# A Mamba layer's inputs computed half by half, with the pair matrix placed by transfers

## The chip, the cores and the metric

The kernel runs on one core of a Trainium2 chip. The metric is the device time of one execution in microseconds, median of the runs shown. Engine names in the rows: PE is TensorE's products and PEld its weight loads, DVE is VectorE, ACT is ScalarE, POOL is GpSimd, SP issues transfers.

## The reference, cut to what matters

The model is a four-layer decoder on x of shape (8, 128, 128), each layer an attention-like part, a cross part and a feed-forward part. The change lies in the first part of the first layer, a Mamba block on the twice-normed x, and in the lines that share its buffers. What it computes, with 256 inner channels, 64 states and a convolution of four taps:

```
xi, z = split(xn @ W_in)                   # 256 channels each
u     = silu(conv4(xi) + conv_b)
dt, B, C = split(u @ W_xproj)              # 8, 64, 64 columns
delta = softplus(dt @ W_dt + b_dt)
A     = -exp(A_log)
h_t   = h_{t-1} * exp(delta_t * A) + (delta_t * u_t) * B_t     # for each channel and state
y_t   = sum over states of h_t * C_t  + u_t * D
out   = (y * silu(z)) @ W_out
```

## The kernel before

Everything runs as blocks: within a block each engine has its own list of instructions, ordered against the others by semaphores written out by hand, and a block ends when all engines have come to its end. There is no planner. Features lie on partitions, the 1024 tokens (8 sequences of 128) on columns; `halves` are 512 columns, one PSUM bank; `IC` is 2, the two groups of 128 channels.

`start_stage` (L251) issues seven loads on SP: X, the Mamba weights `mamba_pack` (1056 KB, the identity among its columns), and five that are needed later (`row_pack`, `CT`, `CTOK`, `rel`, `mask8`). VectorE waits for X and for the whole pack, casts the identity to bf16, and the block ends.

`mamba_stage` (L1006) first norms x twice in one block (`Norm`, L299): VectorE takes statistics and scales, GpSimd takes the power -0.5, TensorE runs bf16 products that nobody reads (`keep_awake`, eight at the first statistics of each norm) and then transposes, VectorE and ScalarE copy one half each into `XNT`.

`mamba_inputs` (L1054) is the block that makes u, gate, delta, du = delta * u, B and C. TensorE's order: four inner products for both halves into banks `Xp` (copied by ScalarE into `padded`, L1148), the second channel group's convolution as four diagonal products a half (`Gp`, L1118), then for each half the dt, B and C products (L1130) and the step products (`Dp`, L1137), and last the gates (L1109 again, into `Gp`). VectorE does the first group's convolution (L1191, L1194) and the softplus, written as max(delta, 0) + ln(1 + e) with a correction. The softplus goes pass by pass over both halves: L1203 twice, then ScalarE's Exp twice (L1172), L1207 twice, Ln twice (L1175), and then L1210, L1213, L1214 and the product with u, L1217, for one half after the other. GpSimd makes the diagonals, adds XN to X (L1227), clears `Cz` (L1228), and builds `A_pairs` (L1231): A times a 0/-1 pattern, so that a product of 32 partitions picks one channel. SP stores du's first half to a scratch tensor in DRAM (L1092), waits, loads the first seven tiles back, spread over partitions (`Spread.load`, L1049, two transfers a tile), and stores the second half.

`scan_block` (L1236) runs 128 tiles, each 128 partitions by 1024. For each: TensorE multiplies delta by `A_pairs` into PSUM (L1331), ScalarE takes Exp (L1445), GpSimd multiplies the loaded du tile by B (L1303), VectorE scans (L1489), and TensorE sums states with `Cz` (L1349). The tiles use a ring of seven areas: `XN`, `XNT`, `O`, `masked_cos`, `masked_sin` and two halves of `pos_bias`. SP loads a tile when the scan seven before it is done. At the end ScalarE widens the mask into `O` (L1457), GpSimd makes the masked tables, and SP loads `pos_bias` (L1291). Later layers use semaphores of their own (`Tally`).

Of the kernel before, what the change touches and what calls it, by code (L numbers as in the profile page):

```python
# [24 lines left out]
T = B * S  # L25
HALF = 512
# [77 lines left out]
def layout(name_shapes):  # L104

    table, at = {}, 0
    for name, n in name_shapes:
# [7 lines left out]
         ("W_out", IC * D), ("pair_rows", 2 * QUADS), ("order", 128), ("alternate", 128)]  # L115
# [25 lines left out]
class Model:  # L141


    def __init__(self, nc, ctx, dram):
# [35 lines left out]
        self.loaded_small = sem("loaded_small")  # L180
# [27 lines left out]
        self.tallies = {}  # L208

    def tally(self, name):  # L210

        if name not in self.tallies:
            self.tallies[name] = Tally(self.sem(f"moe_{name}"))
        self.tallies[name].base = self.tallies[name].n
        return self.tallies[name]
# [35 lines left out]
def start_stage(nc, m):  # L251

    d = m.dram
    with nc.Block() as block:
        @block.sync
        def _(sp):
            sp.dma_start(m.X[:], d["x"]).then_inc(m.loaded_x, 16)
            sp.dma_start(m.mamba_pack[:], d["mamba"]).then_inc(m.loaded_mamba, 16)
            sp.dma_start(m.row_pack[:], d["rows"].to_broadcast([128, ROWS_N])).then_inc(m.loaded_rest, 16)
            sp.dma_start(m.CT[:], d["ctx_feat"]).then_inc(m.loaded_rest, 16)  # L260
            sp.dma_start(m.CTOK[:], d["ctx_tok"]).then_inc(m.loaded_rest, 16)
            sp.dma_start(m.rel[:], d["rel_pos"]).then_inc(m.loaded_rest, 16)
            sp.dma_start(m.mask8[:], d["mask"].to_broadcast([128, T])).then_inc(m.loaded_rest, 16)
# [16 lines left out]
        def _(dve):  # L280
# [8 lines left out]
            dve.wait_ge(m.loaded_mamba, 16)  # L289
            nc.vector.tensor_copy(m.identb[:], m.w("ident"))  # L290

# [7 lines left out]
class Norm:  # L299
# [6 lines left out]
    def __init__(self, nc, m, ctx, src, dst, weight=None, bias=None, ps=None, turn=True):  # L306
        n = m.n_norm
        m.n_norm += 1
        self.turn, self.n_turned = turn, m.n_norm_turned
# [8 lines left out]
    def emit(self, block, complete=None):  # L318
# [48 lines left out]
        def _(pe):  # L367
            pe.wait_ge(m.stats_ready, 2 * n + 1)
            keep_awake(nc, m, ps[:, HALF:], 8)
# [636 lines left out]
def mamba_stage(nc, m):  # L1006

    with ExitStack() as ctx:
        ps = ctx.enter_context(nc.psum_tensor("norm_ps", [D, T], F32))
        first = Norm(nc, m, ctx, m.X, m.XN, ps=ps, turn=False)  # L1010
        second = Norm(nc, m, ctx, m.XN, m.O, m.w("ln_w"), m.w("ln_b"), ps=ps)
        norm_again(m, ctx.enter_context(nc.Block()), first, second)
    with ExitStack() as outer:
        sb = lambda name, shape, dt=F32: outer.enter_context(nc.sbuf_tensor(name, shape, dt))
        u, gate, delta, du = (sb(name, [128, IC, T]) for name in ("u", "gate", "delta", "du"))
        A = sb("A", [128, IC, STATE])
        A_pairs = sb("A_pairs", [128, IC, QUADS, 2, STATE])
        D_order = sb("D_order", [128, IC, 128])
        B2, C2 = sb("B2", [128, T]), sb("C2", [128, T])
        Cz = sb("Cz", [128, S, 32])  # L1020
        du_stored = [m.sem(f"du_stored{h}") for h in range(2)]
        spread = Spread(m)
        mamba_inputs(nc, m, u, gate, delta, du, A, A_pairs, D_order, B2, C2, Cz, du_stored, spread)
        scan_block(nc, m, u, gate, delta, du, A_pairs, D_order, B2, C2, Cz, du_stored, spread)


class Spread:
# [12 lines left out]
    def place(k):  # L1040

        return k // 16, k // 8 % 2, k % 2, k % 8 // 2

# [8 lines left out]


def mamba_inputs(nc, m, u, gate, delta, du, A, A_pairs, D_order, B2, C2, Cz, du_stored, spread):  # L1054
# [5 lines left out]
    with ExitStack() as ctx:  # L1060
# [8 lines left out]
        DTp = ps("DTp", RANK)  # L1069
# [6 lines left out]
        a_ready, diagonal_ready, turned_taps, x_added = (  # L1076
            m.sem(f"mamba_{n}") for n in ("a_ready", "diagonal_ready", "turned_taps", "x_added"))
# [9 lines left out]
        def _(sp):  # L1087
            def store(h):
                sp.wait_ge(du_ready, h + 1)
                for c in range(IC):  # L1090
                    rows = m.dram["du_rows"][h * HB:(h + 1) * HB, c, :, :].rearrange("b r t -> r b t")
                    sp.dma_start(rows, du[:, c, cols[h]].rearrange("r (b t) -> r b t", b=HB)).then_inc(du_stored[h], 16)  # L1092

            store(0)
            sp.wait_ge(x_added, 1)
            sp.wait_ge(g_done, 2 * IC)
            sp.wait_ge(du_stored[0], 16 * IC)
            for k in range(len(spread.areas)):
                spread.load(sp, k)
            store(1)  # L1100

        @block.tensor
        def _(pe):
            def project(ps, at, h, done):
                for c in range(IC):
                    if h:
                        pe.wait_ge(x_copied if at == 0 else g_copied, c + 1)
                    weight = W_in[:, at + c * 128:at + (c + 1) * 128]
                    nc.tensor.matmul(ps[c][:], weight, m.XNT[:, cols[h]], start=True, stop=True).then_inc(done, 1)  # L1109

            for h in halves:
                project(Xp, 0, h, x_done)
            pe.wait_ge(diagonal_ready, TAPS)
            pe.wait_ge(pads_ready, IC)
            for h in halves:
# [5 lines left out]
            for h in halves:  # L1121
# [1589 lines left out]
```

## Time and profile before

| | us |
|---|---|
| median of 3 runs | 1265.73 |
| lowest, highest | 1265.58, 1271.51 |
| span of the profiled execution | 1288.7 |

The span is from the first to the last instruction of the execution that was profiled; of that execution no other time is given. The page shows TensorE busy for 80% of it, VectorE 65%, GpSimd 45% and ScalarE 41%, over stages with different limits, so a stage has to be read by itself. In the rows of a timeline the columns are start, duration, engine, line, operation, output<-inputs, sizes and count, and in brackets the idle time before with what ended it. SPq rows are SP issuing transfers. An f32 product of 512 columns shows as two records.

### The profile page before, as it was taken

The page shows a single profiled execution, that of the slowest core. Times are in us where ns is not written, and L with a number is a line of the kernel's source. Part 1 is how long each engine was busy: PE and PEld are TensorE (multiplying, and loading weights), DVE is VectorE, ACT ScalarE, POOL GpSimd, SP SyncE. Part 2 cuts the span into 40 slices and gives each one's busy share as a digit, 9 for nine tenths or more (in the row PEclk, how much of TensorE's full clock was granted, in tenths as well). Part 3 has the DMA queues.
Part 4 walks back from the last instruction along what each step waited for, and adds up shares of the span by engine and source line. Part 5 has one row for each costly group of instructions (what it writes and reads, how often), then busy time and mean ns, then how long its engine had stood idle before and what let it go on. Part 6 is the DMA issues. An engine that isn't in the chain of part 4 may idle for free. (4 is left out here: it accounts for less than half of the span.)

```text
span 1288.7 us, 30057 instructions
## 1 busy us (share of the span) xinstructions
PE 1028.3 (80%) x12227; PEld 718.2 (56%) x12237; DVE 841.0 (65%) x1508; ACT 525.7 (41%) x1329; POOL 574.0 (45%) x393
## 2 busy tenths in 40 slices
PE   6538877887889999998365798899497999957895
PEld 2127666666774555555265355655377455533795
DVE  5469999999896775567322787487322788855233
ACT  2534444444443742552132274175144577502121
POOL 3389999999964613101435310110524321002232
PEclk9859999999899999999588899899689899978898
DMA  2198899998875000000473000000465000003792
GB/s 114 45 226 213 233 232 230 224 223 228 211 224 190 2 1 1 1 2 1 114 205 110 20 2 1 1 1 2 162 183 192 1 2 2 1 1 95 254 305 83
DMA packets 74376, 139.77 MB, mean 108 GB/s; under 512 B 8144, under 2 KB 28384, under 8 KB 73888
## 3 DMA queue, kind: packets, MB, share of 16 engines
q1 hardware_dynamic: 70272, 129.67, 36.0%
q0 software_dynamic: 3968, 8.18, 1.8%
q8 instruction: 97, 1.59, 0.5%
q14 instruction: 39, 0.32, 0.1%
HBM read 128.06 MB, written 14.82 MB: 111 GB/s over the span
## 5 line engine op out<-in xcount | busy, mean ns | idle before, releaser
L888 ACT ACTIVATE shifted_a<-scores,nmax_a 128x128 f32<-128x128 f32 x768 | 208.6, 389 | 77.4 <-DVE nmax_a L832 75.9
L1445 ACT ACTIVATE decay<-decay 128x1016 f32<-128x1016 f32 x128 | 124.0, 1002 | 152.5 <-PE decay L1331 152.4
L832 DVE TENSOR_REDUCE nmax_a<-scores 128x4 f32<-128x512 f32 x192 | 123.6, 686 | 69.6 <-PE scores L718 67.4
L364 POOL TENSOR_TENSOR rstd<-ve,neghalf 128x4 f32<-128x4 f32 x30 | 31.5, 1051 | 255.9 <-DVE ve L349 255.9
L1331 PE MATMUL decay<-delta,A_pairs 32*128 32x127 f32 x2048 | 83.3, 300 | 75.4 <-DVE small_pack L1489 34.0
L1785 POOL DMA_INDIRECT results<-xs_s x76 | 72.9, 960 | 120.9 <-DVE xs_s L1960 114.5
L838 DVE COPY PTs_a<-PT 128x512 f32<-128x512 f32 x192 | 123.1, 682 | 2.6 <-PE PT L728 2.6
L1331 PEld LDWEIGHTS decay<-delta,A_pairs 32*128 32x128 f32 x2048 | 69.7, 201 | 94.9 <-DVE small_pack L1489 39.4
L728 PE MATMUL PT<-mamba_pack,shifted_a 128*128 128x128 f32 x768 | 106.3, 280 | 4.4 <-DVE PTs_a L838 2.6
L728 PEld LDWEIGHTS PT<-mamba_pack,shifted_a 128*128 128x128 f32 x768 | 82.3, 141 | 30.3 <-issue 19.2
L1303 POOL TENSOR_TENSOR pos_bias<-pos_bias,B 128x1024 f32<-128x1024 f32 x36 | 85.4, 2407 | 1.9 <-DMA pos_bias<-du_rows 1.9
L718 PE MATMUL scores<-KH_a,QT_a 32*128 32x512 f32 x256 | 72.1, 640 | 0.0
L674 POOL TENSOR_TENSOR KH_a<-KT_a,small_pack 128x512 f32<-128x512 f32 x24 | 25.3, 1060 | 99.4 <-PE scores L718 87.6
L1349 PE MATMUL Y<-h,Cz 128*32 128x64 f32 x2048 | 62.1, 288 | 2.9 <-issue 2.1
L1349 PE MATMUL Y<-small_pack,Cz 128*32 128x64 f32 x2048 | 62.4, 288 | 1.4 <-issue 1.4
L1960 DVE TENSOR_SCALAR xs_s<-Y_s,xs_s 128x128 f32<-128x128 f32 x76 | 25.9, 348 | 55.2 <-PE Y_s L1822 26.4
L747 PEld LDWEIGHTS PO<-PTs_a,V 128*32 128x32 f32 x1280 | 30.1, 109 | 53.6 <-DVE PTs_a L838 28.7
L1349 PEld LDWEIGHTS Y<-h,Cz 128*32 128x32 f32 x2048 | 55.1, 125 | 6.7 <-issue 3.1
L1349 PEld LDWEIGHTS Y<-small_pack,Cz 128*32 128x32 f32 x2048 | 55.2, 125 | 5.3 <-issue 2.5
L1303 POOL TENSOR_TENSOR XN<-XN,B 128x1024 f32<-128x1024 f32 x19 | 45.8, 2409 | 27.0 <-POOLq L1060 27.0
L248 PE MATMUL norm_ps<-identb 128*128 128x512 bf16 x68 | 23.9, 477 | 34.6 <-DVE ve L349 34.6
L747 PE MATMUL PO<-PTs_a,V 128*32 128x128 f32 x1280 | 51.5, 279 | 0.0
(482 smaller groups left out, 2272.5 us busy)
## 6 DMA issues: line engine op xcount, KB each, us to landing
pos_bias<-du_rows SPq DMA_DIRECT2D x72, 256.0 KB, 5.2
small_pack<-L3f_w SPq DMA_DIRECT2D x15, 768.0 KB
XN<-du_rows SPq DMA_DIRECT2D x38, 256.0 KB, 5.0
XNT<-du_rows SPq DMA_DIRECT2D x38, 256.0 KB, 5.0
O<-du_rows SPq DMA_DIRECT2D x36, 256.0 KB, 5.0
masked_cos<-du_rows SPq DMA_DIRECT2D x36, 256.0 KB, 5.0
masked_sin<-du_rows SPq DMA_DIRECT2D x36, 256.0 KB, 5.3
small_pack<-L2f_w SPq DMA_DIRECT2D x15, 514.0 KB
```

The costliest lines, as they stand in the source:

```text
L364: nc.gpsimd.tensor_tensor(rstd[:, bs], ve[:, bs], m.neghalf[:, bs], ALU.pow).then_inc(m.rstd_ready, 1)
L718: nc.tensor.matmul(scores[u % 4], QT[rows, b % B * S:(b % B + 1) * S], KH[b % 2][rows, :, :], start=False, stop=True).then_inc(m.scored, 1)
L728: t = nc.tensor.transpose(PT[u % 2][:, j, :], shifted[u % 4][:, j, :], ident)
L747: t = nc.tensor.matmul(PO[32 * j:32 * j + 32, g, :], values[:, b % B, g * HG + j, :], PTs[u % 4][:, j, :], start=True, stop=True)
L832: nc.vector.tensor_reduce(nmax[:, u % 4, :], scores[u % 4], AX.X, ALU.min).then_inc(m.maxed, 1)
L838: nc.vector.tensor_copy(PTs[u % 4][:], PT[u % 2]).then_inc(m.pt_copied, 1)
L888: t = nc.scalar.activation(shifted[u % 4][:, j, :], scores[u % 4][:, j, :], ACT.Exp, scale=-1.0, bias=nmax[:, u % 4, j:j + 1])
L1303: nc.gpsimd.tensor_tensor(x, x, bcast_mid(B2[:, b * S:(b + 1) * S], PER), ALU.mult).then_inc(fed, 1)
L1331: t = nc.tensor.matmul(decay[(2 * p + side) % DEEP][:, s, i, 1:S], A_pairs[strip, c, 4 * q + i, :, :].rearrange("p j n -> p (j n)"), delta ...
L1349: t = nc.tensor.matmul(Y[32 * i:32 * i + 32, n % 2, half, :], Cz[:, token, :], at_token[n % 2][:, :, token], start=(turn % 16 == 0), stop= ...
L1445: nc.scalar.activation(x, x, ACT.Exp).then_inc(decayed, 1)
L1785: nc.gpsimd.indirect_dma_start(results, bass.IndirectOffsetOnAxis(ap=number, axis=0), xs[:, j, 0:D], None).then_inc(returned.sem, returned ...
```

## The change

- `start_stage` loads X, the identity and the rest of the Mamba pack; VectorE waits for X and the identity. The five other loads go out on SP in the norm block (`load_rest`). VectorE waits for the pack before the second norm. The second norm has three keep-awake products in place of eight.
- In the norm block ScalarE fills `A_pairs` and `Cz` with zeros and takes A = Exp(A_log).
- In the inputs block SP places A into `A_pairs` by 32 transfers of four partitions each, ahead of du's store. GpSimd's fill of `Cz` and its two multiplies go. The minus sign of A moves into the scan's Exp (`scale=-1.0`), and TensorE waits for the 32 transfers before the scan's first product.
- The inputs are computed half by half: TensorE's and ScalarE's orders are rewritten, the gates of half 0 go into the banks `Dp` early and those of half 1 into a bank `Gx`, and VectorE does half 0's whole softplus before half 1's. The Exp and Ln tables are loaded for each half, and Exp's once more at the block's end.
- GpSimd multiplies the scan's first two tiles by B within the inputs block. The ring's order of areas becomes `O`, the halves of `pos_bias`, `masked_cos`, `masked_sin`, `XN`, `XNT`. du's second store moves to the start of the scan block. The mask and the bias table wait for the last scans of their new places.
- Semaphores that are done with are used again by the later layers' tallies, at their value; three of those layers' semaphores become shared tallies.

Cut to its core:

```diff
 start_stage, sync:
             sp.dma_start(m.X[:], d["x"]).then_inc(m.loaded_x, 16)
-            sp.dma_start(m.mamba_pack[:], d["mamba"]).then_inc(m.loaded_mamba, 16)
-            sp.dma_start(m.row_pack[:], d["rows"].to_broadcast([128, ROWS_N])).then_inc(m.loaded_rest, 16)
...
+            sp.dma_start(m.w("ident"), d["mamba"][:, 0:128]).then_inc(m.loaded_ident, 16)
+            sp.dma_start(m.mamba_pack[:, 128:], d["mamba"][:, 128:]).then_inc(m.loaded_mamba, 16)
 start_stage, vector:
-            dve.wait_ge(m.loaded_mamba, 16)
+            dve.wait_ge(m.loaded_ident, 16)
 mamba_stage, the norm block:
+            second = Norm(nc, m, ctx, m.XN, m.O, m.w("ln_w"), m.w("ln_b"), ps=ps, awake=3)
+            def _(sp):
+                load_rest(sp, m)
+            def _(act):
+                zeros = m.neghalf[:, 0:1].to_broadcast([128, IC * 2 * QUADS * STATE])
+                nc.scalar.activation(A_pairs[:].rearrange("p c i n -> p (c i n)"), zeros, ACT.Copy, scale=0.0)
+                zeros = m.neghalf[:, 0:1].to_broadcast([128, S * 32])
+                nc.scalar.activation(Cz[:].rearrange("p t i -> p (t i)"), zeros, ACT.Copy, scale=0.0)
+                act.wait_ge(m.loaded_mamba, 16)
+                nc.scalar.activation(A[:].rearrange("p c n -> p (c n)"), m.w("A_log"), ACT.Exp)
+            def _(dve):
+                dve.wait_ge(m.loaded_mamba, 16)
 Spread:
-        areas = [flat(m.XN[:]), m.XNT[:], flat(m.O[:]), flat(m.masked_cos[:]), flat(m.masked_sin[:]),
-                 flat(m.pos_bias[:, 0:H // 2, :]), flat(m.pos_bias[:, H // 2:, :])]
+        areas = [flat(m.O[:]), flat(m.pos_bias[:, 0:H // 2, :]), flat(m.pos_bias[:, H // 2:, :]),
+                 flat(m.masked_cos[:]), flat(m.masked_sin[:]), flat(m.XN[:]), m.XNT[:]]
 mamba_inputs, sync:
+            for row in range(32):
+                q, j, r = row // 8, row // 4 % 2, row % 4
+                sp.dma_start(A_pairs[row:128:32, :, (4 * q + r) * 2 + j, :], A[row:128:32, :, :]
+                             ).then_inc(pairs_placed, 16)
+            sp.wait_ge(du_ready, 1)
+            spread.store(sp, du, 0, du_stored[0])
             sp.wait_ge(du_stored[0], 16 * IC)
             for k in range(len(spread.areas)):
+                if k == 5:
+                    sp.wait_ge(x_added, 1)
+                if k == 6:
+                    sp.wait_ge(g_done, 2 * IC)
                 spread.load(sp, k)
-            store(1)
 mamba_inputs, tensor (the new order):
+            inner(0)
+            gate_of(0, 0, Dp[0])
+            gate_of(0, 1, Dp[1])
+            inner(1)
+            pe.wait_ge(diagonal_ready, TAPS)
+            pe.wait_ge(pads_ready, IC)
+            taps(0)
+            reduce(DTp, 0, 0, RANK, dt_done)
+            gate_of(1, 0, Gx)
+            steps_of(0)
+            pe.wait_ge(x_copied, 2 * IC)
+            reduce(Xp[0], 0, RANK, 128, b_done)
+            taps(1)
+            reduce(Xp[1], 0, RANK + 128, 128, c_done)
+            pe.wait_ge(g_copied, 3)
+            gate_of(1, 1, Gx)
+            reduce(DTp, 1, 0, RANK, dt_done)
+            steps_of(1)
+            pe.wait_ge(b_copied, 1)
+            reduce(Xp[0], 1, RANK, 128, b_done)
+            pe.wait_ge(c_copied, 1)
+            reduce(Xp[1], 1, RANK + 128, 128, c_done)
 mamba_inputs, scalar (the new order, after the four copies into padded):
+            silu(0)             # conv half, then gate_of(0, 0, Dp[0]), then the taps half
+            gate_of(0, 1, Dp[1])
+            copy_low(0)
+            gate_of(1, 0, Gx)
+            add_steps(0)
+            exp(0)
+            copy_b(0)
+            log(0)
+            silu(1)
+            copy_c(0)
+            gate_of(1, 1, Gx)
+            copy_low(1)
+            add_steps(1)
+            exp(1)
+            copy_b(1)
+            log(1)
+            copy_c(1)
+            m.load_table(act, ACT.Exp)
 mamba_inputs, vector (softplus(h) is L1203 to L1217 for one half):
+            for h in halves:
+                taps(h)
+            for h in halves:
+                softplus(h)
 mamba_inputs, gpsimd:
-            nc.gpsimd.memset(Cz[:], 0.0)
...
-                nc.gpsimd.tensor_tensor(A_pairs[:, c, :, :, :].rearrange("p i j n -> p (i j) n"),
-                                        bcast_mid(A[:, c, :], 2 * QUADS), bcast_last(m.w("pair_rows"), STATE), ALU.mult)
+            pool.wait_ge(b_copied, 1)
+            for k in range(EARLY):             # EARLY = 2
+                spread.multiply(nc.gpsimd, k, B2, fed)
 scan_block:
+            spread.store(sp, du, 1, du_stored[1])
...
-            sp.wait_ge(scanned, free(6))
+            sp.wait_ge(scanned, max(free(1), free(2)))
...
+            for k in range(EARLY, TILES):
+                spread.multiply(nc.gpsimd, k, B2, fed)
...
+            pe.wait_ge(pairs_placed, 16 * 32)
...
-                    nc.scalar.activation(x, x, ACT.Exp).then_inc(decayed, 1)
+                    nc.scalar.activation(x, x, ACT.Exp, scale=-1.0).then_inc(decayed, 1)
...
-                    act.wait_ge(scanned, free(2))
+                    act.wait_ge(scanned, free(0))
```

## Rows read from the trace of the kernel before

**Rows 1.** Span of the core and its mean granted TensorE clock.
```profile
core 0: 1288.7 us, clock 0.916
```

**Rows 2.** Busy time by stretch: PE, PEld, DVE, ACT, POOL; granted clock, DMA share, GB/s.
```profile
30.00:45.00 15.00, 15.00 (x34) 5.02 (x34) 3.54 (x1) 6.93 (x12) 12.17 (x5) 1.00 0.00 0
45.00:54.00 9.00, 1.67 (x4) 0.38 (x2) 6.40 (x7) 8.91 (x10) 0.00 (x0) 0.79 0.00 0
58.00:69.20 11.20, 0.00 (x0) 0.00 (x0) 1.90 (x2) 0.22 (x2) 0.03 (x1) 0.61 0.77 186
```

**Rows 3.** Order of time, the start and the end of the norm block.
```profile
0.75 0.39 SPq L257 DMA_DIRECT2D X<-x  x1
...
3.47 0.91 DVE L287 MEMSET k_mask<- 1x1024 bf16 x1 [0.16 <-issue]
...
7.18 0.23 DVE L290 CAST identb<-mamba_pack 128x128 bf16<-128x128 f32 x1 [2.80 <-DMA mamba_pack<-mamba]
...
18.34 0.78 ACT L333 ACTIVATE XNT<-norm_ps,mamba_pack 128x512 f32<-128x512 f32 x1 [9.38 <-PE norm_ps L372]
```

**Rows 4.** Transfers of the first 75 us: size of each, median us to landing.
```profile
mamba_pack<-mamba SPq DMA_DIRECT2D x1, 1056.0 KB, 5.9
...
XN<-du_rows SPq DMA_DIRECT2D x3, 256.0 KB, 4.6
...
X<-x SPq DMA_DIRECT2D x1, 512.0 KB, 3.4
...
masked_sin<-du_rows SPq DMA_DIRECT2D x2, 256.0 KB, 8.6
```

**Rows 5.** Order of time, the inputs block: TensorE, ScalarE and VectorE.
```profile
23.02 7.03 PE L1118 MATMUL Gp<-padded,diagonal 128*128 128x512 f32 x16
...
23.22 0.60 ACT L1148 ACTIVATE padded<-Xp 128x512 f32<-128x512 f32 x1 [0.26 <-PE Xp L1109]
23.83 1.28 ACT L1152 ACT_TABLE_LOAD   x1
...
37.44 0.69 ACT L1168 ACTIVATE delta<-Dp,mamba_pack 128x512 f32<-128x512 f32 x1 [0.17 <-PE Dp L1137]
...
46.79 2.00 ACT L1172 ACTIVATE small_pack<-small_pack 128x1024 f32<-128x1024 f32 x2
...
48.83 0.69 DVE L1207 TENSOR_SCALAR small_pack<-small_pack 128x1024 f32<-128x1024 f32 x1 [0.25 <-ACT small_pack L1172]
...
53.80 1.22 DVE L1217 TENSOR_TENSOR du<-delta,u 128x1024 f32<-128x1024 f32 x1
```

**Rows 6.** Order of time, the inputs block: GpSimd and VectorE beside each other.
```profile
37.00 3.62 POOL L1231 TENSOR_TENSOR A_pairs<-A,mamba_pack 128x2048 f32<-128x2048 f32 x1
38.16 3.54 DVE L1203 SCALAR_TENSOR_TENSOR small_pack<-delta 128x1024 f32<-128x1024 f32 x1 [11.17 <-ACT delta L1168]
...
40.60 1.57 POOL L1233 TENSOR_SCALAR D_order<-mamba_pack 128x128 f32<-128x128 f32 x1
...
45.51 1.23 DVE L1203 SCALAR_TENSOR_TENSOR small_pack<-delta 128x1024 f32<-128x1024 f32 x1 [3.81 <-ACT delta L1168]
```

**Rows 7.** Order of time, SP's issues in the inputs block.
```profile
55.05 0.94 SPq L1092 DMA_DIRECT2D du_rows<-du  x2
58.36 1.34 SPq L1049 DMA_DIRECT2D XN<-du_rows  x2
...
67.59 1.14 SPq L1092 DMA_DIRECT2D du_rows<-du  x2
```

**Rows 8.** Order of time, the scan: its first, one late, and the last of both engines.
```profile
72.56 2.29 DVE L1489 TENSOR_TENSOR_SCAN small_pack<-decay,XN 128x1024 f32<-128x1024 f32 x1 [2.87 <-ACT decay L1445]
...
339.18 2.29 DVE L1489 TENSOR_TENSOR_SCAN small_pack<-decay,XN 128x1024 f32<-128x1024 f32 x1 [2.39 <-ACT decay L1445]
...
368.84 2.38 POOL L1303 TENSOR_TENSOR XNT<-XNT,B 128x1024 f32<-128x1024 f32 x1
...
374.50 2.27 DVE L1489 TENSOR_TENSOR_SCAN h<-decay,XNT 128x1024 f32<-128x1024 f32 x1
```

More of the change, by code:

```diff
@@ L299, with __init__ @@
 class Norm:
-    def __init__(self, nc, m, ctx, src, dst, weight=None, bias=None, ps=None, turn=True):
+    def __init__(self, nc, m, ctx, src, dst, weight=None, bias=None, ps=None, turn=True, awake=8):
         n = m.n_norm
         m.n_norm += 1
+        self.awake = awake
         self.turn, self.n_turned = turn, m.n_norm_turned
@@ L1006, in mamba_stage @@
 def mamba_stage(nc, m):
[L1008 to L1012, printed above, removed]
     with ExitStack() as outer:
         sb = lambda name, shape, dt=F32: outer.enter_context(nc.sbuf_tensor(name, shape, dt))
+        A, A_pairs = sb("A", [128, IC, STATE]), sb("A_pairs", [128, IC, 2 * QUADS, STATE])
@@ new lines, in mamba_stage @@
+        Cz = sb("Cz", [128, S, 32])
+        pairs_placed = m.sem("pairs_placed")
+        with ExitStack() as ctx:
+            ps = ctx.enter_context(nc.psum_tensor("norm_ps", [D, T], F32))
+            first = Norm(nc, m, ctx, m.X, m.XN, ps=ps, turn=False)
+            second = Norm(nc, m, ctx, m.XN, m.O, m.w("ln_w"), m.w("ln_b"), ps=ps, awake=3)
+            block = ctx.enter_context(nc.Block())
+            @block.sync
+            def _(sp):
+                load_rest(sp, m)
+            @block.scalar
+            def _(act):
[5 more added lines that the diff above has]
+                nc.scalar.activation(A[:].rearrange("p c n -> p (c n)"), m.w("A_log"), ACT.Exp)
+            first.emit(block)
+            @block.vector
+            def _(dve):
+                dve.wait_ge(m.loaded_mamba, 16)
+            second.emit(block, lambda dve, half: (m.normed, first.n * B + 4 * half + 4))
@@ L1042, in place, with store @@
         return k // 16, k // 8 % 2, k % 2, k % 8 // 2
+    def store(self, sp, du, h, stored):
+        batches = slice(h * (B // 2), (h + 1) * (B // 2))
+        for c in range(IC):
+            sp.dma_start(self.rows[batches, c, :, :].rearrange("b r t -> r b t"),
+                         du[:, c, h * HALF:(h + 1) * HALF].rearrange("r (b t) -> r b t", t=S)).then_inc(stored, 16)
     def load(self, sp, k):
@@ L1087, in _, with inner, taps @@
         def _(sp):
[L1088 to L1096, printed above, removed]
+            for row in range(32):
[4 more added lines that the diff above has]
+            spread.store(sp, du, 0, du_stored[0])
             sp.wait_ge(du_stored[0], 16 * IC)
             for k in range(len(spread.areas)):
+                if k == 5:
+                    sp.wait_ge(x_added, 1)
+                if k == 6:
+                    sp.wait_ge(g_done, 2 * IC)
                 spread.load(sp, k)
-            store(1)
         @block.tensor
         def _(pe):
-            def project(ps, at, h, done):
+            def inner(h):
                 for c in range(IC):
                     if h:
[L1107 to L1115, printed above, removed]
+                        pe.wait_ge(x_copied, c + 1)
+                    nc.tensor.matmul(Xp[c][:], W_in[:, c * 128:(c + 1) * 128], m.XNT[:, cols[h]], start=True, stop=True
+                                     ).then_inc(x_done, 1)
+            def taps(h):
                 pe.wait_ge(x_copied, (h + 1) * IC)
@@ L1183, in _, with taps @@
             steps = m.dve_steps
-            dve.wait_ge(pads_ready, IC)
-            for h in halves:
+            at = lambda a, h: a[:, :, cols[h]]
+            def taps(h):
                 out = conv[:, cols[h]].rearrange("p (b s) -> p b s", b=HB)
```

161 lines of the change are left out of this document (82 added, 79 removed).

## The prediction

> **What bounds the kernel now.** I read the times and the span first. The profiled execution spans 1288.7 us [rows 1], 23.0 us above the median of 1265.73, so a saving read from it is worth 1265.7/1288.7 = 0.982 of itself. The chain of work that ended last covers only the last stage and says nothing of the change, so I took the busy time by stretches, then the order of time, engine by engine, over the first 75 us, then the scan's two ends. Times below are of the profiled execution, from its span's start.
>
> Four stretches matter. (1) The start: VectorE's cast of the identity waits at 7.18 us for the whole Mamba pack [rows 3]. (2) The inputs block, 19.4 to 68.7 us. From 30 to 45 us TensorE is busy for 15.00 of 15.00 us while VectorE does 3.54 us; from 45 to 54 us ScalarE and VectorE work alone; from 58 to 69.2 us almost only transfers run (VectorE 1.90 us, TensorE nothing) [rows 2]. Nothing of u times delta goes out before both halves' logarithms are done. (3) The block ends when SP has issued its last store, 67.59 + 1.14 = 68.7 us [rows 7], and the first scan is at 72.56 [rows 8]. (4) The scan is VectorE's: the last GpSimd product ends at 368.84 + 2.38 = 371.2, the last scan begins at 374.50 [rows 8], so GpSimd is 3.3 us ahead at the end.
>
> **The start.** X is issued at 0.75 and lands 3.4 us later, 4.15 us [rows 3, 4]; VectorE's own memsets end at 3.47 + 0.91 = 4.38. The pack lands 5.9 us after its issue [rows 4]. The identity alone is an eighth of X's bytes and goes out right behind X. Its landing isn't shown: not before 4.4 (the memsets), not after 7.2 (the pack). I take 4.6, near X, since it is small and queued next: **-2.6 us**, bounds 0 and -2.8. The five later loads are issued in the norm block, where SP has nothing else to do; their first reader is the scan block.
>
> ScalarE's new work there: two fills of 4096 columns and one Exp. A 512-column copy is 0.60 us, a 1024-column Exp 1.00 [rows 5], so 0.8 us more for each 1024: 3.4 us for 4096 columns. With a table load of 1.28 it is about 8.4 us, from 5.1 to 13.5. ScalarE was idle for 9.38 us there, and its next work (18.34, now about 15.7) still comes 2.2 us later [rows 3]. Cost 0; if the fills ran at half that rate they would add 4.6. Five fewer bf16 keep-awake products shorten nothing VectorE waits for; what they may do to the clock is a rival below.
>
> **The inputs block, half 0.** A 512-column f32 product takes 7.03/8 = 0.88 us [rows 5]. TensorE now runs six of them first (two inner, two gates, two inner): 19.4 + 5.3 = 24.7, so the last input copy ends at 25.4, where it ended at 23.8. Table load 1.28 and first silu 0.63: 27.3; a gate's silu 0.6: 27.9. The four taps end at 28.2, the second silu at 29.0. The second dt product 0.88, its copy 0.6, two step products 1.8, the second bias 0.69: 33.4, against 37.44 + 0.69 = 38.1 before [rows 5]. Then, without waiting for half 1: VectorE 1.23 (its Exp table load lies beside this), Exp 1.0, VectorE 0.69 [rows 5]: 36.5; the B copy and the Ln table hold ScalarE until 37.7, Ln ends at 38.7, three VectorE passes of 1.22 end at **42.5**. Before, half 0's product ended at 53.80 + 1.22 = 55.0 [rows 5].
>
> **Half 1.** ScalarE from 38.7: silu table 1.28, two silus, C copy, gate, dt copy: 43.2. Two step products and the biases: 46.0. Exp table 1.28, Exp 1.0: 48.5; B copy and Ln table: 50.3; Ln: 51.3; three passes: 55.1, were VectorE alone. TensorE is done by 48.6, ScalarE by 53.2.
>
> **SP's queue.** The 32 small transfers of the pair matrix stand ahead of du's store. One issue costs 0.39 (X, one run to a partition [rows 3]) to 0.67 (a tile's load [rows 7]): 12.5 to 21.4 us, done by 31.9 to 40.8, under the cover of the 23.1 us until 42.5. That breaks at 0.72 us each; beyond it, 3.2 us for every 0.1. The store goes out at 42.6; the loads began 58.36 - 55.05 = 3.3 us behind it [rows 7], so at 45.9. Fourteen issues at (67.59 - 58.36)/14 = 0.66: 55.1. The waits for the residual sum and the last gate come before the sixth and seventh tile and are over by 41. TensorE's new wait, for the 32 landings, stands ahead of the scan's first product, some 20 us after they are due; GpSimd's for the B copy (36.5) has only the two products behind it, which need tile 0 anyway. Half 1's store moves into the scan block, in front of a load that waits for the first scan; its 1.1 us are covered there.
>
> **GpSimd's two early products.** Tile 0 lands 4.6 us after its issue, tile 4 after 8.6 [rows 4], so a tile lands each 1.3 + 1.0 = 2.3 us: 50.5 and 52.8. Two products of 2.35 (the same operation as the last one, 2.38 [rows 8]). They meet VectorE's three passes of half 1. What that costs, the trace shows once: a VectorE pass with two SBUF inputs took 3.54 us instead of 1.23 and ended 1.08 us after the GpSimd multiply beside it (37.00 + 3.62 = 40.62), and GpSimd's next step was stretched to 1.57 in its turn [rows 6]. One at a time, 3 x 1.22 + 2 x 2.35 = 8.4 us from 50.5: **58.9**. Side by side it would be 55.3. I take 58.9: the row is of the same pair of engines and operand kinds. (The Trainium skill, "SBUF — State Buffer", section "Who interferes with whom", has the rule: a VectorE instruction with two SBUF inputs and a GpSimd one that reads SBUF lock each other out. The row agrees; it speaks against putting the early products here.) They gain nothing: the first scan waited for ScalarE's decay [rows 8], and so it will.
>
> **Sum.** Block end 68.7 to 58.9: **-9.8**. GpSimd's fill of Cz and two multiplies of 3.62 [rows 6] go, but lay beside other work: 0. Table loads go from five to seven up to the first scan, counted above at 1.28. (The Trainium skill, "ScalarE: Activation LUTs", section "What ACT_TABLE_LOAD costs", adds a drain of about 1.38 us to each switch. In the trace the load starts at 23.83, 0.01 us after a copy ends [rows 5], so no drain shows. By the page five switches on the path to 55.1 would add 6.9 us, an estimate, and leave about -6.7 in all.) The scan block begins as before, with idle TensorE ahead of it. In its tail the mask waits for tile 126's scan instead of tile 121's, and ScalarE came there in order after it; the bias table goes out 2 us later and is read a stage later: 0. The negated scale and the reused semaphores: 0. Total -2.6 - 9.8 = -12.4, times 0.982 = -12.2: **1253.5 us**.
>
> **Rivals.**
> *No collision*: the products lie after VectorE's passes or beside them without a lock. Block end 55.3, -16.0 in all, 1250.0. Against: the two windows overlap by the sum above. 0.20.
> *No gain at the start*: the identity lands with the pack. -9.6, 1256.1. 0.10.
> *SP becomes the bound*: the small transfers cost 1.0 us each on the queue, 32 x 0.28 = 9.0 us past the cover, nearly all on the loads behind. -3.4, 1262.4. Against: X, which has sixteen times the runs of a small transfer, was issued in 0.39 [rows 3]. 0.08.
> *Given back in the scan or behind*: TensorE's granted clock falls to 1.2 GHz at places that depend on when work is issued; one such place cost VectorE 2.39 us before one scan [rows 8]. Three more like it leave -5.2, 1260.6. Nothing ties them to the change, so they could as well go. 0.10.
> *Slower: the clock falls in the inputs block.* Five of eight products that keep TensorE busy before the second norm's transposes go. If the clock were at 1.2 GHz from 19.4 on, the 32 products would take 1.76 us each, TensorE would set every step, and the same chain ends at 79.5 instead of 58.9: +10.8 - 2.6 = +8.2, 1273.8. It decides once about three fifths of the block ((71.3 - 58.9)/(79.5 - 58.9)) run at the low level. Against: TensorE then is almost never idle, and its clock was 1.00 in the stretch where it never stopped; it was lower where it mostly stood (0.79 from 45 to 54 us, with 1.67 us of work [rows 2]). 0.05.
>
> **How the numbers follow.** The forecast has 0.47. Differences within 0.5% (6.3 us, about what a measurement of this kernel can tell) are the SP case and *given back*, 0.18, of which 0.01 goes to both at once with the clock case: 0.17; slower is then 0.06; faster is the rest, 0.77. The range goes from *no collision* with a little of luck (1247.5) to past *given back* (1261.5); outside it are the SP case, the clock case and the tails.
>
> **What would show it.** Right: the identity's cast near 4.6; du's first store near 40 us (42.6 - 2.6); 32 issues done before it; VectorE passes of half 1 stretched above 2 us beside the two GpSimd products; first scan near 60.2 us; the scan's length unchanged within 3 us; the last GpSimd product still ahead of the last scan. Wrong: SP still issuing small transfers when du is ready; a granted clock below 1 between 17 and 45 us; GpSimd waiting for tile 0 beyond 50 us; a scan that starts earlier and ends no earlier.

## The result and the profile after

The kernel after takes 1257.93 us (median of 4 runs, 1256.44 to 1258.97); the kernel before, run beside it, 1266.55 (4 runs, 1265.58 to 1271.51). The ratio is 0.992 with a 95% interval of 0.9891 to 0.9949: faster by 0.5 to 1.1%. The forecast was 1253.5 with a range of 1247.5 to 1261.5, so the direction and the range hold and the gain came out at 8.6 us instead of 12.2. By the interval the gain is 6.5 to 13.8 us, which takes in the forecast. The profiled execution took 1258.97 us, its span 1257.3, so 1.7 us lie around the span. One execution of the kernel before, in a later round, took 1941.43 us, far from all the others, and is left out of every comparison below.

First the stretches of the kernel after (columns as in [rows 2]), the inputs block and the passage to the scan:

```profile
30.00:45.00 15.00, 14.30 (x33) 5.29 (x32) 7.58 (x7) 12.74 (x16) 0.00 (x0) 1.00 0.13 37
45.00:54.00 9.00, 2.11 (x5) 0.57 (x3) 6.82 (x5) 6.35 (x8) 4.69 (x2) 0.76 0.91 217
54.00:61.00 7.00, 2.61 (x34) 1.92 (x34) 3.71 (x6) 1.87 (x4) 4.36 (x3) 0.50 1.07 229
```

Against [rows 2], VectorE does 7.58 us beside TensorE's work from 30 to 45 us instead of 3.54, and the transfers (DMA share 0.91) run from 45 us on, where they stood at 0.00. The empty stretch of before, 11 us of almost nothing but transfers, is gone.

Then the order of time of the kernel after, all engines, from the start to the scan's end:

```profile
4.40 0.23 DVE L288 CAST identb<-mamba_pack 128x128 bf16<-128x128 f32 x1
...
11.54 1.46 PE L250 MATMUL norm_ps<-identb 128*128 128x512 bf16 x3 [1.47 <-DVE ve L358]
...
13.87 0.42 PE L381 MATMUL norm_ps<-mamba_pack,O 128*128 128x128 f32 x1
...
17.34 18.58 SPq L1135 DMA_DIRECT2D A_pairs<-A  x32
17.39 1.95 PE L1153 MATMUL Xp<-XNT,mamba_pack 128*128 128x512 f32 x4 [1.11 <-PEq L1022]
...
31.03 0.69 ACT L1224 ACTIVATE delta<-Dp,mamba_pack 128x512 f32<-128x512 f32 x1 [0.17 <-PE Dp L1177]
31.74 1.28 ACT L1237 ACT_TABLE_LOAD   x1
33.03 1.06 ACT L1237 ACTIVATE small_pack<-small_pack 128x1024 f32<-128x1024 f32 x1
...
39.57 1.22 DVE L1306 TENSOR_TENSOR du<-delta,u 128x1024 f32<-128x1024 f32 x1
...
40.82 0.95 SPq L1078 DMA_DIRECT2D du_rows<-du  x2
44.07 1.34 SPq L1086 DMA_DIRECT2D O<-du_rows  x2
...
49.31 2.34 POOL L1094 TENSOR_TENSOR O<-O,B 128x1024 f32<-128x1024 f32 x1 [20.23 <-DMA O<-du_rows]
49.52 3.21 DVE L1302 TENSOR_TENSOR small_pack<-small_pack 128x1024 f32<-128x1024 f32 x1 [0.97 <-ACT small_pack L1241]
51.61 3.32 POOL L1094 TENSOR_TENSOR pos_bias<-pos_bias,B 128x1024 f32<-128x1024 f32 x1
51.95 1.25 SPq L1086 DMA_DIRECT2D XNT<-du_rows  x2
52.77 3.24 DVE L1303 SCALAR_TENSOR_TENSOR delta<-delta,small_pack 128x1024 f32<-128x1024 f32 x1
56.05 1.23 DVE L1306 TENSOR_TENSOR du<-delta,u 128x1024 f32<-128x1024 f32 x1
...
61.05 2.29 DVE L1586 TENSOR_TENSOR_SCAN small_pack<-decay,O 128x1024 f32<-128x1024 f32 x1 [2.95 <-ACT decay L1542]
...
66.64 2.29 DVE L1586 TENSOR_TENSOR_SCAN small_pack<-decay,pos_bias 128x1024 f32<-128x1024 f32 x1 [1.11 <-ACT decay L1542]
...
72.14 2.29 DVE L1586 TENSOR_TENSOR_SCAN small_pack<-decay,masked_sin 128x1024 f32<-128x1024 f32 x1 [1.03 <-ACT decay L1542]
...
355.97 2.51 POOL L1094 TENSOR_TENSOR pos_bias<-pos_bias,B 128x1024 f32<-128x1024 f32 x1
...
360.61 2.27 DVE L1586 TENSOR_TENSOR_SCAN h<-decay,pos_bias 128x1024 f32<-128x1024 f32 x1
```

Read down, each step of the prediction has its row: the cast at 4.40 instead of 7.18 [rows 3]; 32 small transfers issued by 17.34 + 18.58 = 35.9, well ahead of du's first store at 40.82 (55.05 before [rows 7]); two VectorE passes stretched to 3.21 and 3.24 beside the two GpSimd products; the last load issued by 53.2 instead of the store's end at 68.7; the block's end now set by VectorE, at 57.28. The first scan starts at 61.05 instead of 72.56 [rows 8], and the last at 360.61 instead of 374.50.

### The profile page after: what moved, and what is told of

Read it like the earlier page. It is cut to its first block and busy times, and to the rows that moved or that the text cites. A ratio compares the mean times of both kernels' runs of the same rounds, so it can differ in the third digit from the quotient of the medians.

```text
span 1257.3 us, 30097 instructions
## 1 busy us (share of the span) xinstructions
PE 1019.8 (81%) x12232; PEld 712.5 (57%) x12232; DVE 845.9 (67%) x1508; ACT 535.0 (43%) x1334; POOL 563.9 (45%) x390
## 5 line engine op out<-in xcount | busy, mean ns | idle before, releaser
L1094 POOL TENSOR_TENSOR pos_bias<-pos_bias,B 128x1024 f32<-128x1024 f32 x37 | 89.3, 2453 | 5.0 <-POOLq L1106 2.6
L1094 POOL TENSOR_TENSOR O<-O,B 128x1024 f32<-128x1024 f32 x19 | 46.4, 2440 | 20.5 <-DMA O<-du_rows 20.5
L1997 ACT ACTIVATE silu_s<-G_s 128x512 f32<-128x512 f32 x30 | 17.9, 597 | 79.3 <-PE U_s L1910 63.5
```

Source lines behind the costliest of these rows:

```text
L1094: pool.tensor_tensor(x, x, bcast_mid(B2[:, b * S:(b + 1) * S], 8), ALU.mult).then_inc(fed, 1)
```

## The experiments

**Both kernels again, unchanged.** No edit. The profile of before spans 23 us more than its median: is that the changed part, or chance elsewhere? And is the head start at the first scan kept to the end?

> The kernel before, unchanged, profiled and timed once more. The profiled executions of before and after differ by 31.4 us in span, the medians by 8.6. Theory A (the part ahead of the L1 feed-forward is the same in every execution, and the profiled execution of before was slow by chance behind it): first scan again at 72.6 us, the norm after the scan at 384 us, within 3 us of the profile of before, and a span nearer 1265 than 1289. Theory B (the later layers of before are really slower than those of after): the span again near 1288, and the expert layer from 606 us on again some 13 us longer than in after.

> The changed kernel, unchanged, timed in more rounds beside before. Theory A (what the first two blocks and the scan save, 13.9 us at the scan's end in the profiles, reaches the end): ratio near 0.990, -12 to -14 us. Rival (a part of it is given back behind the scan): ratio 0.993 or above, -9 us or less, and in the profile the shift against before shrinks somewhere behind the scan.

Before: 1267.29 us (12 runs, 1260.75 to 1273.42), span 1265.3, ratio to the same kernel beside it 0.9985 (0.9958 to 1.0011). After: 1258.46 (6 runs, 1252.97 to 1259.57), span 1257.4, ratio 0.9909 (0.9878 to 0.9941). In order of time, VectorE in before's first profile (a norm behind the scan, and one two layers on):

```profile
603.87 0.87 DVE L343 BATCH_NORM_STATS2 stats<-X 128x6 f32<-128x128 f32 x4
...
998.97 0.87 DVE L343 BATCH_NORM_STATS2 stats<-X 128x6 f32<-128x128 f32 x4
```

and in the repeated run of before, the identity's cast, the scan's two ends and the same two norms:

```profile
6.84 0.23 DVE L290 CAST identb<-mamba_pack 128x128 bf16<-128x128 f32 x1 [2.45 <-DMA mamba_pack<-mamba]
...
72.15 2.29 DVE L1489 TENSOR_TENSOR_SCAN small_pack<-decay,XN 128x1024 f32<-128x1024 f32 x1 [2.87 <-ACT decay L1445]
...
372.64 2.26 DVE L1489 TENSOR_TENSOR_SCAN h<-decay,XNT 128x1024 f32<-128x1024 f32 x1
...
600.92 0.87 DVE L343 BATCH_NORM_STATS2 stats<-X 128x6 f32<-128x128 f32 x4
...
975.06 0.87 DVE L343 BATCH_NORM_STATS2 stats<-X 128x6 f32<-128x128 f32 x4
```

The first scan moved by 0.4 us between the two executions, the norm at 604 us by 2.9, the one at 999 by 23.9. The excess lay behind the changed part, so scaling the saving by 0.982 had no ground. The repeated run of after, in order of time:

```profile
61.40 2.29 DVE L1586 TENSOR_TENSOR_SCAN small_pack<-decay,O 128x1024 f32<-128x1024 f32 x1 [2.95 <-ACT decay L1542]
...
361.14 2.26 DVE L1586 TENSOR_TENSOR_SCAN h<-decay,pos_bias 128x1024 f32<-128x1024 f32 x1
```

After is 10.75 us ahead at the first scan and 11.5 at the last. Behind the scan the lead moves both ways: 13.9 us at the norm at 600.92 us (587.07 in after), 10.2 at the one at 975.06 (964.90) and 7.9 at the spans' end (1265.3 - 1257.4). The median of before beside it is 1268.18 (16 runs), 9.7 us more than after's; the ratio gives 11.5. That lies between the theory's 12 to 14 us and the rival's 9 or less, so the head start reaches the end at least for the most part, and whether some of it is given back behind the scan stays open.

**Without the two early products.**

```diff
-EARLY = 2
+EARLY = 0
```

> The changed kernel with EARLY = 0: GpSimd multiplies no tile in the inputs block, the scan block multiplies all 128. Theory (the two products and VectorE's three last passes exclude each other, and the products buy nothing): the passes of half 1 take 1.22 each instead of 3.21 and 3.24, the inputs block ends at 53.4 instead of 57.3, the first scan is 3.9 us earlier at 57.2 and waits for ScalarE's decay as before; 3 to 4 us faster than the changed kernel. Rival (the head start is worth its price): the first scans or the last ones wait for GpSimd's products, and the time is equal to or above that of the changed kernel.

1253.25 us (6 runs, 1250.66 to 1255.01), ratio 0.9872 (0.9844 to 0.9901). Order of time, VectorE and SP:

```profile
49.21 1.22 DVE L1302 TENSOR_TENSOR small_pack<-small_pack 128x1024 f32<-128x1024 f32 x1 [0.97 <-ACT small_pack L1241]
50.47 1.23 DVE L1303 SCALAR_TENSOR_TENSOR delta<-delta,small_pack 128x1024 f32<-128x1024 f32 x1
51.68 1.27 SPq L1086 DMA_DIRECT2D XNT<-du_rows  x2
51.72 1.22 DVE L1306 TENSOR_TENSOR du<-delta,u 128x1024 f32<-128x1024 f32 x1
...
57.11 2.29 DVE L1586 TENSOR_TENSOR_SCAN small_pack<-decay,O 128x1024 f32<-128x1024 f32 x1 [2.96 <-ACT decay L1542]
```

The passes are 1.22 again and the first scan starts 3.9 us earlier than in after. The wait ahead of it is 2.96 us for ScalarE's decay, as with the early products (2.95): they save nothing there and cost 4 us. This version is 5.2 us under after's repeated median, in the same round. Its trace alone would not show that: its scan is 304.8 us long against after's 301.8, so at the scan's end only 1.0 us of the lead is left (361.86 against 362.88). The five waits at the scan's start are the same; those behind them come to 7.2 us instead of 4.4, all of them for ScalarE's decay and none for GpSimd. Such later waits come to 4.2 to 8.8 us in the six traces with early products and to 7.2 in both that have neither early products nor the busy TensorE of the last two runs, so whether the early products have a part in them stays open. SP's last issue (52.95) and VectorE's last pass (52.94) now end together, so more from VectorE alone would bring nothing.

**Eight keep-awake products again.**

```diff
-            second = Norm(nc, m, ctx, m.XN, m.O, m.w("ln_w"), m.w("ln_b"), ps=ps, awake=3)
+            second = Norm(nc, m, ctx, m.XN, m.O, m.w("ln_w"), m.w("ln_b"), ps=ps, awake=8)
```

> The changed kernel with eight keep-awake products at the second norm again, in place of three. Theory (with three the granted clock falls before the transposes: they took 0.42 us a record instead of 0.27): the transposes take 0.27 again, the inputs block's first product comes at 16.6 instead of 17.4 us, 0.8 us faster than the changed kernel. Rival (the clock was low there for another reason, the fill of the norm block or the shifted start): still 0.42, no difference.

1255.68 us (6 runs, 1250.39 to 1261.70), ratio 0.9901 (0.9865 to 0.9938): not to be told from after. Its order of time on TensorE, the last transposes and the first product:

```profile
14.28 0.27 PE L381 MATMUL norm_ps<-mamba_pack,O 128*128 128x128 f32 x1
...
16.65 1.95 PE L1153 MATMUL Xp<-XNT,mamba_pack 128*128 128x512 f32 x4 [1.11 <-PEq L1022]
```

and its stretch of 30 to 45 us (columns as in [rows 2]):

```profile
30.00:45.00 15.00, 14.32 (x28) 5.35 (x28) 6.82 (x6) 11.65 (x15) 0.00 (x0) 0.86 0.13 36
```

A transpose takes 0.27 us instead of after's 0.42, and the inputs block starts 0.74 us earlier. But in this execution the clock stood at 0.86 in the block, where after had 1.00, and the first scan came at 61.02: the gain was gone. Two later runs, one the same as after and one the same as this run up to the end of the norm block, show that the number of products doesn't settle the transposes' time. The one with 64 transfers has three:

```profile
13.88 0.27 PE L381 MATMUL norm_ps<-mamba_pack,O 128*128 128x128 f32 x1
...
16.63 1.96 PE L1154 MATMUL Xp<-XNT,mamba_pack 128*128 128x512 f32 x4 [1.11 <-PEq L1022]
```

The one with eight and no early products runs its eight at the low level, 0.44 us each instead of 0.24, and its first product comes at 17.93:

```profile
11.60 3.49 PE L250 MATMUL norm_ps<-identb 128*128 128x512 bf16 x8 [1.47 <-DVE ve L358]
```

From the cast to the inputs block's first product it is 12.2 to 13.3 us in seven traces with three products, 12.2 to 13.8 in three with eight, and 12.2 in both of before. One trace of each kind can't tell what the five products are worth.

**The start of before**, with `load_rest` back in the first block and out of the norm block.

```diff
-            sp.dma_start(m.w("ident"), d["mamba"][:, 0:128]).then_inc(m.loaded_ident, 16)
-            sp.dma_start(m.mamba_pack[:, 128:], d["mamba"][:, 128:]).then_inc(m.loaded_mamba, 16)
+            sp.dma_start(m.mamba_pack[:], d["mamba"]).then_inc(m.loaded_mamba, 16)
+            load_rest(sp, m)
...
-            dve.wait_ge(m.loaded_ident, 16)
+            dve.wait_ge(m.loaded_mamba, 16)
```

> The changed kernel with the start of before: one load of the whole Mamba pack, VectorE waits for it, and the five other loads go out in the first block. Theory (the start is worth the 2.4 to 2.8 us by which the cast comes earlier, and nothing behind hides it): cast at 6.8 to 7.2 instead of 4.40 us, inputs block and first scan later by the same, 2.5 us slower than the changed kernel. Rival (the rest of the changed kernel hides it, since the norm block's clock or ScalarE's fills set its end): first scan less than 1 us later.

1258.36 us (6 runs, 1254.87 to 1261.53), ratio 0.9929 (0.9904 to 0.9954). The cast is at 6.83 and the first scan at 63.58, 2.5 us behind after's and 2.2 behind its repeat's. The trace shows the start's worth nearly as predicted (2.6); the medians don't (after's repeat has 1258.46), and they can't tell 2.5 us.

**The pair matrix by GpSimd again**, with the pattern positive, and without the 32 transfers and ScalarE's fill of `A_pairs`.

```diff
-            for row in range(32):
-                q, j, r = row // 8, row // 4 % 2, row % 4
-                sp.dma_start(A_pairs[row:128:32, :, (4 * q + r) * 2 + j, :], A[row:128:32, :, :]
-                             ).then_inc(pairs_placed, 16)
...
+                nc.gpsimd.tensor_tensor(A_pairs[:, c, :, :], bcast_mid(A[:, c, :], 2 * QUADS),
+                                        bcast_last(m.w("pair_rows"), STATE), ALU.mult).then_inc(pairs_placed, 1)
```

> The changed kernel with the pair matrix made by GpSimd's two multiplies in the inputs block again (positive pattern), without the 32 transfers and without ScalarE's fill of it. Theory (a GpSimd multiply and a VectorE pass with two SBUF inputs exclude each other): GpSimd's multiplies, 3.6 us each from 27.9 us, stretch half 0's passes; du's first store comes 1.5 to 4 us later than 40.8 and the first scan as much. Rival (the 32 issues on SP's queue cost more than they spare): the first scan is as early or earlier.

1256.22 us (6 runs, 1255.71 to 1262.06), ratio 0.9921 (0.9898 to 0.9944): as after. First scan at 61.96, 0.9 us later than after's, and 0.56 later than in its repeat. Order of time, GpSimd and VectorE:

```profile
31.72 4.40 POOL L1322 TENSOR_TENSOR A_pairs<-A,mamba_pack 128x2048 f32<-128x2048 f32 x1
...
33.78 2.88 DVE L1291 TENSOR_SCALAR small_pack<-small_pack 128x1024 f32<-128x1024 f32 x1 [1.14 <-ACT small_pack L1231]
```

The multiply and a VectorE pass met again, at a cost of 2.2 us to the pass (0.69 alone), of which 1.2 reach the first scan, counted from the inputs block's first product (17.06; after's 17.39). du's first store goes out at 41.78, less late than the 1.5 to 4 us expected. In the trace, placing the matrix by transfers is worth that much here, no more; the medians don't show it.

**Twice as many small transfers**, each of half the size.

```diff
-                sp.dma_start(A_pairs[row:128:32, :, (4 * q + r) * 2 + j, :], A[row:128:32, :, :]
-                             ).then_inc(pairs_placed, 16)
+                for c in range(IC):
+                    sp.dma_start(A_pairs[row:128:32, c, (4 * q + r) * 2 + j, :], A[row:128:32, c, :]
+                                 ).then_inc(pairs_placed, 16)
```

> The changed kernel with 64 transfers of half the size in place of the 32. Theory (an issue costs 0.58 us whatever its bytes, and the 32 end 4.9 us before du is ready): SP issues until 54.5 us, du's store goes out then, 13.7 us later; tile 0 lands near 63, VectorE's passes take 1.22 again, GpSimd's two products end the block at 67.6 and the first scan is at 71.4, 10 us slower than the changed kernel. Rival (the cost goes with the bytes): SP is done at 36 us and nothing changes.

1264.89 us (10 runs, 1260.58 to 1268.36), ratio 0.9986 (0.9967 to 1.0004): not to be told from before, though the first scan still starts 3.6 us earlier than before's (72.56). Order of time, SP and VectorE:

```profile
16.57 34.80 SPq L1136 DMA_DIRECT2D A_pairs<-A  x64
51.42 0.98 SPq L1078 DMA_DIRECT2D du_rows<-du  x2
...
68.98 2.29 DVE L1587 TENSOR_TENSOR_SCAN small_pack<-decay,O 128x1024 f32<-128x1024 f32 x1 [2.96 <-ACT decay L1543]
```

34.80/64 = 0.54 us for an issue of half the bytes, against 18.58/32 = 0.58: SP's time goes by the count. The store waits for the last issue, and all behind it is late: the first scan by 7.9 us against after's, where 10 were expected. The rival "SP becomes the bound" was real; after is 40.82 - 35.92 = 4.9 us short of it.

**No early products and eight keep-awake ones** (both edits above).

> The changed kernel without early products and with eight keep-awake products at the second norm. Theory (the two parts add): inputs block's first product at 16.6, first scan at 56.3, 4.7 us earlier than in the changed kernel; 0.5 to 1 us faster than without early products alone. Rival (the earlier start is taken back in the scan): scan longer by 3 us, as in the profile of the run without early products, where it took 304.8 against 301.8 us.

1252.91 us (6 runs, 1246.14 to 1258.21), ratio 0.9883 (0.9849 to 0.9917). First scan at 59.85, where 56.3 was expected: the two parts did not add. In this execution the eight keep-awake products took 3.49 us (1.90 in the run with eight of them and the early products), and the clock stood at 0.89 from 30 to 45 us. Up to the end of the norm block those two runs are the same program, so there TensorE's level differs by chance from execution to execution; of the 2.7 us between this first scan and the one with three keep-awake products (57.11), 0.9 are there at the inputs block's first product (17.93 and 17.07).

**Busy TensorE at the scan's start.** In every profile above, of before and after, VectorE waits five times for about 1.05 us in the scan's first 28 us (two of them are the rows at 66.64 and 72.14 of after). There a decay product, which serves two tiles, takes 2.09 us, later 1.17. These two runs put bf16 products that nobody reads before and between the first decay products, on the two versions without early products (with three keep-awake products, then with eight).

```diff
             reduce(Xp[1], 1, RANK + 128, 128, c_done)
+            keep_awake(nc, m, Gp[0][:], 24)
...
+                if 0 < p < 5:
+                    for _ in range(14):
+                        nc.tensor.matmul(YT[:, 2:4, :], m.identb[:], m.q_mask[:, 0:2 * S], start=True, stop=True)
```

> The kernel after without the two early products, and with bf16 products that nobody reads: 24 at the end of the inputs block's TensorE list and 14 behind each of the second to fifth decay product of the scan. In every run so far VectorE waits five times for about 1.05 us (5.3 us in all) within the first 28 us of the scan, while TensorE's granted clock is at 1.2 GHz and a tile's decay product takes 2.09 us instead of 1.17. Theory (the scan's start pays for TensorE at the low level): the clock is at 2.4 GHz from the first scan or soon after, the decay products there take 1.17 us, the five waits together fall below 1.5 us, and the time is some 4 us under that of the kernel without early products alone (1253.3), near 1249. Rival (the waits come from the products' order, not from the clock): five waits of about 1 us stay, time within 2 us of 1253. Second rival (TensorE's clock falls at other places of the scan instead): the five waits go, but as much appears later in the scan, whose length stays at 302 us or more.

> The same bf16 products as in the run before it, on the kernel without early products and with eight keep-awake products in the second norm. Theory (the scan's start pays for TensorE at the low level): the five waits of about 1.05 us fall below 1.5 us together and the time comes out some 4 us under 1252.9, near 1249. Rival: five waits of about 1 us stay, time within 2 us of 1253. First scan between 56.3 and 60 us by either, since the norm block varies from execution to execution.

With three: 1253.71 us (6 runs, 1249.22 to 1257.25), ratio 0.9878 (0.9840 to 0.9917). With eight: 1248.88 us (6 runs, 1246.45 to 1253.64), ratio 0.9845 (0.9808 to 0.9882). Order of time of the first of them:

```profile
55.06 1.17 PE L1428 MATMUL decay<-delta,A_pairs 32*128 32x127 f32 x32 [0.78 <-DVE decay L1579]
...
66.64 2.29 DVE L1590 TENSOR_TENSOR_SCAN small_pack<-decay,masked_sin 128x1024 f32<-128x1024 f32 x1
...
71.23 2.29 DVE L1590 TENSOR_TENSOR_SCAN small_pack<-decay,XNT 128x1024 f32<-128x1024 f32 x1
```

and the same in the run without them (the one without early products):

```profile
53.96 2.09 PE L1427 MATMUL decay<-delta,A_pairs 32*128 32x127 f32 x32 [7.17 <-DVE decay L1575]
...
68.20 2.29 DVE L1586 TENSOR_TENSOR_SCAN small_pack<-decay,masked_sin 128x1024 f32<-128x1024 f32 x1 [1.03 <-ACT decay L1542]
...
73.70 2.29 DVE L1586 TENSOR_TENSOR_SCAN small_pack<-decay,XNT 128x1024 f32<-128x1024 f32 x1 [1.03 <-ACT decay L1542]
```

The stretch from 57 to 85 us, without them and with them (columns as in [rows 2]):

```profile
57.00:85.00 28.00, 11.72 (x209) 10.38 (x212) 22.57 (x11) 10.26 (x13) 28.00 (x13) 0.50 0.84 221
...
57.00:85.00 28.00, 17.80 (x326) 13.98 (x326) 26.91 (x13) 12.10 (x14) 28.00 (x14) 0.93 1.07 245
```

The granted clock is 0.93 instead of 0.50. Two tiles take 4.59 us instead of 5.50, the difference of the two product times (2.09 - 1.17 = 0.92). Of the five waits 0.27 us are left, with eight keep-awake products one of 1.11, since there the first two decay products still take 2.09. The scan is 299.3 and 298.3 us long instead of 304.8 and 304.1. So the five waits come from TensorE's low level, as the theory said. The scan's gain is not their sum alone, since later waits differ as well, and another engine becomes its limit. Order of time of the run with eight, GpSimd and VectorE:

```profile
353.50 2.39 POOL L1094 TENSOR_TENSOR pos_bias<-pos_bias,B 128x1024 f32<-128x1024 f32 x1
...
355.99 2.29 DVE L1590 TENSOR_TENSOR_SCAN h<-decay,pos_bias 128x1024 f32<-128x1024 f32 x1
```

The last scan starts 0.10 us after the last GpSimd product ends (355.89). In after that product was 2.1 us ahead, and 4.2 without the early products. GpSimd's 128 products follow each other without a wait here, from 56.47 to 355.89, and take 299.4 us; with three keep-awake products it is 299.5. With TensorE busy, then, the scan ends at GpSimd's pace, and products done early, which bought nothing before, might be worth something there. No run tests that.

Of the time's part of the theory only the second run bears out 4 us; the first gave nothing. In its trace the lead of 5.2 us at the end of the scan is 6.2 at 450 us, 2.2 to 2.5 from 784 us on and 0.3 at the end of the span: lost at places in later layers that the edit doesn't touch. Over the twelve runs with and the twelve without these products the means are 1251.6 and 1252.9, so how much of the 5.4 and 5.8 us is left at the end stays open. The version with eight has the lowest median here, 9.6 us under after's repeated one, though the two were measured in separate rounds; by their ratios to before it is 8.1 us.

## Why the prediction was right, and where it was off

**The start** was right at the cast (4.40; forecast 4.6) and off behind it. The step that was off is "Five fewer bf16 keep-awake products shorten nothing VectorE waits for": it puts TensorE's level in the norm block at nothing, but VectorE waits for the transposes there, and these ran at 0.42 us instead of 0.27. The first product came at 17.39, 2.02 us earlier than before's (19.41) and not 2.78 as the cast did. The term is 0 to 1.1 us in the seven traces with three products (12.2 to 13.3 us from cast to first product, against 12.2 in before). That the five dropped products are its cause isn't shown: eight took it away in one trace (by 0.74 us) and not in two others, and one trace with three was without it.

**The inputs block** was right. From its first product to the end of half 0's du it took 40.79 - 17.39 = 23.4 us; the forecast was 23.1 (its steps up to the second bias add up to 33.0, not to the 33.4 it goes on from, and they took 0.8 us more than those steps). Half 1 without the early products ended 52.94 - 17.07 = 35.9 us behind the first product; the forecast for VectorE alone was 55.1 - 19.4 = 35.7. Table loads cost 1.28 us each and nothing else: the load at 31.74 starts 0.02 us after an activation ends, the next activation 0.01 us after the load. (The Trainium skill, "ScalarE: Activation LUTs", section "What ACT_TABLE_LOAD costs", adds a drain of about 1.38 us to a switch. None shows, and had there been one on each of the switches on the path, du would have come later than it did; the measurement decides. The "-6.7 in all" of the prediction's estimate is the block's part alone, 68.7 - 55.1 - 6.9; with the start's 2.6 it is -9.3.)

**SP** was right: 0.58 us an issue, inside the bounds of 0.39 and 0.67, and the run with 64 shows the price beyond the cover. From store to load it took 3.25 us (forecast 3.3).

**The collision** was right in mechanism and nearly in size: from the first GpSimd product to the end of the last pass 57.28 - 49.31 = 7.97 us, forecast 8.4. That the sum came out so near is partly luck: from tile 0's issue to that product it took 49.31 - 44.07 = 5.24 us and not 4.6, and the two misses nearly cancel. The rows tell how: the first pass ends at 52.73, 1.08 us after the product beside it (51.65); the second product, begun meanwhile, takes 3.32 instead of 2.34; the second pass ends at 56.01, again 1.08 after it (54.93). That is the 1.08 of [rows 6]. The run without the products gives the loss, 3.9 us. (The Trainium skill, "SBUF — State Buffer", section "Who interferes with whom", says that a VectorE instruction with two SBUF inputs contends with a GpSimd one that reads SBUF, and that a `tensor_scalar` in a mode with two ports does too. The first shows here. The stretched one-input pass of the GpSimd variant fits the second; that it ran in such a mode is an inference from its 0.69 us, where passes with two inputs take 1.22.) "They gain nothing" was right for this kernel: the first scan waits for decay with them and without, and GpSimd is ahead at the scan's end. With TensorE kept busy it need not hold.

**The scan** kept its length (304.2 and 302.8 us before, 301.8 and 302.0 after), and the head start was kept to its end, so "given back in the scan" is out. Behind it the lead moves by several us both ways (13.9, 10.2 and 7.9 us in the repeats), and a part given back there is not excluded.

**The sum.** Forecast -12.4 at the block's end. The traces give -11.5 at the first scan (61.05 against 72.56) and -10.75 between the repeats. Of the 0.9 missing in the first pair the start has 0.6 (2.02 instead of 2.6) and the block 0.4 (9.4 instead of 9.8). The factor of 0.982 did little harm (0.2 us), but its reason was wrong: the execution's extra 23 us lay in later layers. The medians moved by 8.6 us and, in the second round, by 1268.18 - 1258.46 = 9.7. Single executions of before spread over 12.7 us in that round, so whether the 1 to 3 us between these and the traces' lead were lost behind the scan can't be told.

## What to carry to other kernels

Work put early into an idle engine must be checked against what runs beside it: two products that nobody needed yet cost 4 us at the first scan, because GpSimd and VectorE held each other up. Whether such a lead is worth its price depends on which engine sets the pace of the stage behind it, and that can change with the next edit. Many tiny transfers are cheap only while their issue time, by the count, fits under a cover that can be named. Where a filler product is dropped or added, look at the next few products of TensorE and at the start of the next long stage, and in more than one execution.

## What was not expected of the hardware

- The scan begins with TensorE at 1.2 GHz for some 28 us in every profile without fillers (granted clock 0.50 from 57 to 85 us in the row above), and VectorE, which bounds that scan, waits 5.3 us for it. With TensorE kept busy ahead of and between the first decay products most of that stretch ran at 2.4 GHz (0.93), and all but 0.3 or 1.1 us of these waits went; the scan then ended at GpSimd's pace.
- A VectorE pass with one input was held up by GpSimd as well: 2.88 us instead of 0.69, ending 0.54 us after the multiply beside it (36.12).
- An issue on SP cost 0.54 to 0.58 us for transfers of 1 or 2 KB, more than for X with 512 KB (0.39).
- The same program had an execution 23 us over its median, almost all of it behind the changed part; a saving is better read between landmarks of two traces than scaled by the span.
